# Order by destination stored without gaps, its gathers in a ring of 64 chunks: a four-layer graph network

## What is computed

```python
# layer 0: three hops, z = segment_sum(edge_weight * z[src], dst as rows) ...
# layer 1: 8 heads, softmax over the edges of each dst
e = (q[dst] * kt[edge_type, src]).sum(-1) * ...
a = softmax of e per dst;  agg = segment_sum(a * vt[edge_type, src], dst)
# layer 2: 4 heads, softmax per dst of att . leaky_relu(x_l[src] + x_r[dst])
out = segment_sum(alpha * x_l[src], dst)
# layer 3: 8 heads, scores q[src] . k[dst], softmax per src, sum per dst
weights = softmax of scores per src;  agg = segment_sum(v[src] * weights, dst)
```

## Time and profile before

| what | value |
|---|---|
| median of 3 runs | 13384.99 us (13377.65 to 13407.79) |
| profiled execution, span | 13177.8 us |
| its own time | not listed apart from the span; the median lies 207.2 us over the span |
| TensorE's mean granted clock | 0.635 of full speed |
| first gather of layer 1, 2, 3, weighing pass | 6900.7, 8566.2, 10202.1, 11693.4 us |
| last gather of the same | 8385.2, 10067.5, 11573.7, 13120.0 us |
| gathers of the same | 832, 832, 784, 832 |

### The profile page before, as it was taken

One profiled execution on the slowest core, in us unless ns is written; L12 is line 12 of the kernel. 1 busy time (PEld: TensorE's weight loads), 2 busy tenths in 40 slices (PEclk: granted clock), 3 DMA queues, 4 the chain that ended last, 5 costly groups with the idle time before them and its releaser, 6 DMA issues. The chain is left out here.

```text
span 13177.8 us, 169349 instructions
## 1 busy us (share of the span) xinstructions
PE 6872.9 (52%) x37679; PEld 6012.4 (46%) x37680; DVE 6549.5 (50%) x22663; ACT 2082.2 (16%) x6208; POOL 7027.7 (53%) x7417
## 2 busy tenths in 40 slices
PE   5555444445554555100384555656666566665555
PEld 4444333335554555100234455456665465654444
DVE  6444455555555555200265555755556344455555
ACT  4222100001110111000121111311222111122222
POOL 6555566646664666777205555245553555535554
PEclk6555555556666666555687777877787555556766
DMA  0000011111111111010143222111112211112232
GB/s 19 1 1 1 21 44 44 44 42 42 42 43 40 42 42 43 16 22 8 50 157 79 74 74 74 56 38 39 39 39 65 52 38 38 38 47 77 79 81 74
DMA packets 436083, 614.60 MB, mean 47 GB/s; under 512 B 176625, under 2 KB 312133, under 8 KB 435173
## 3 DMA queue, kind: packets, MB, share of 16 engines
q0 software_dynamic: 257024, 486.93, 14.5%
q1 hardware_dynamic: 178369, 119.49, 3.2%
q10 hardware_dynamic: 292, 3.41, 0.1%
HBM read 520.17 MB, written 89.19 MB: 46 GB/s over the span
## 5 line engine op out<-in xcount | busy, mean ns | idle before, releaser
L1094 POOL DMA_INDIRECT hop_rows<-hops,k_src_gather x1568 | 1479.3, 943 | 1077.3 <-issue 435.9
L1137 PE MATMUL hop_sums<-hop_rows,hop_weighted 128*128 x4992 | 1159.9, 405 | 1110.7 <-DVE k_x L1184 736.1
L1137 PEld LDWEIGHTS hop_sums<-hop_rows,hop_weighted 128*128 128x128 f32 x4992 | 1009.7, 300 | 1201.7 <-issue 1200.4
L1443 POOL DMA_INDIRECT l_pass_rows<-related,k_dst_typed x832 | 786.2, 945 | 1216.8 <-POOLq L74 517.6
L1443 POOL DMA_INDIRECT l_pass_rows<-left_table,k_dst_other x832 | 786.6, 945 | 895.7 <-DVE l_pass_terms L1815 490.5
L1938 POOL DMA_INDIRECT l_weigh_rows<-row_table,l_weigh_ring x832 | 813.0, 977 | 733.8 <-ACT l_weigh_ring L1902 466.3
L1443 POOL DMA_INDIRECT l_pass_rows<-key_table,k_src_gather x784 | 739.5, 943 | 766.6 <-DVE l_pass_scores L1752 387.3
L726 POOL DMA_INDIRECT src_sorted<-src_scatter_records,src_scatter_places x784 | 750.6, 957 | 606.3 <-DVE src_scatter_places L714 393.6
L1538 PE MATMUL l_pass_sums<-l_pass_zero 128*128 128x272 bf16 (+1 forms) x1210 | 262.7, 306 | 1454.0 <-DVE l_total L1632 1005.2
L1094 POOL DMA_INDIRECT hop_rows<-in_x,k_src_gather x784 | 739.6, 943 | 456.4 <-issue 220.8
L1292 POOL DMA_INDIRECT dst_sorted<-rec,dst_places x784 | 809.2, 1032 | 262.1 <-issue 262.1
(11 more groups left out here) (467 smaller groups left out, 18342.8 us busy)
## 6 DMA issues: line engine op xcount, KB each, us to landing
related<-l_tables_rows SPq DMA_DIRECT2D x50, 1024.0 KB, 4.4
hop_rows<-hops,k_src_gather POOLq DMA_INDIRECT x1568
l_pass_rows<-related,k_dst_typed POOLq DMA_INDIRECT x832
l_pass_rows<-left_table,k_dst_other POOLq DMA_INDIRECT x832
l_weigh_rows<-row_table,l_weigh_ring POOLq DMA_INDIRECT x832
src_sorted<-src_scatter_records,src_scatter_places POOLq DMA_INDIRECT x784
hop_rows<-in_x,k_src_gather POOLq DMA_INDIRECT x784
dst_sorted<-rec,dst_places POOLq DMA_INDIRECT x784
```

Source lines behind the costliest of these rows:

```text
L1094: nc.gpsimd.indirect_dma_start(rows[:, s * G + g, :], None, table_in, bass.IndirectOffsetOnAxis(ap=o.gather[:, c:c + 1], axis=0),).then_in ...
L1137: last = nc.tensor.matmul(sums[:, b, g, :], weighted[:, s % SLOTS, g, :], rows[:, bass.ds(slots[g], 1), :], start=True, stop=True)
L1443: nc.gpsimd.indirect_dma_start(rows[:, s, g, :], None, table, bass.IndirectOffsetOnAxis(ap=index[:, c:c + 1], axis=0),).then_inc(got[s], 16)
```

## The change

The order by destination is placed by `place_edges` too, without gaps, and read by a new `read_sorted`, which picks place and begins of the columns by masks. Layers 1 and 2 and the weighing pass then gather 784 chunks into a ring of 16 batches. Chunks of a group are no longer neighbours in the ring, so each engine that reads them loads four places and works chunk by chunk: DVE for pairs, terms and the weighing pass's subtraction, ACT for layer 2's copy, PE for layer 2's matmul with the gathered rows. The waits on `got` become waits on `landed` by a loaded count. `o.release` holds, for each batch, after how many groups its ring place is free; POOL loads it and waits for that many terms. In the weighing pass POOL's loop is unrolled, ACT's copy of indices goes, and SP is added. Layer 3's softmax pass and the hops stay as they are. The diff, cut to its core:

```diff
--- before.py
+++ after.py
@@ place_edges, tensor @@
+        if o.release is not None:
...
@@ place_edges, vector (its end) @@
+        if o.release is not None:
+            chain(nc.vector.tensor_scalar(bound[:], o.chunk_no[0:TU, 0:2], float(G), float(G), ALU.mult, ALU.add))
+            below = column_no[0:TU, :]
+            for h in range(2):
...
+            dve.wait_ge(pe_step, 5)
+            chain(nc.vector.tensor_scalar(upto_i[:], upto_rows, float(G - 1), None, ALU.add))
+            nc.vector.tensor_single_scalar(o.release, upto_i[96:97, :], 2, ALU.arith_shift_right)
@@ read_sorted (new, in place of read_order), tensor @@
+            for h in range(2):
+                pe.wait_ge(loaded[h], 16)
+                for f, out, done in ((1, turned, other_ok), (2, typed, typed_ok)):
+                    for q in range(here_q):
+                        last = nc.tensor.transpose(out[:, h, q * TU:(q + 1) * TU], by_edge[:, h * here_q + q, :, f],
+                                                   k.ident[0:TU, 0:TU])
+                    last.then_inc(done, 1)
+            pe.wait_ge(chosen_ok, 1)
+            pick_columns(nc, placed, zero, lambda q: by_edge[:, q, :, 0], chosen).then_inc(placed_ok, 1)
+            pe.wait_ge(found, 2)
+            pick_columns(nc, begun, zero, lambda q: starts[:, q, :], chosen).then_inc(begun_ok, 1)
...
@@ read_sorted, vector: 8 of these, then the fields @@
+                last = nc.vector.tensor_scalar(chosen[:, q, 0:hi - TU * q], o.chunk[0:TU, TU * q:hi], o.chunk_no[0:TU, q:q + 1],
+                                               None, ALU.is_equal)
+            last.then_inc(chosen_ok, 1)
...
@@ -1317,10 +1281,9 @@
-    ring = lag + 1 if values_at is not None else RING if ringed else 4
     with ExitStack() as ctx:
         sb, ps, sem = tools(nc, k, ctx, name)
-        rows = sb("rows", [P, ring, G, row])
+        rows = sb("rows", [P, RING * G, row])
@@ softmax_pass, sync @@
-            for n in range(GU if ringed else 0):
+            for n in range(GU):
                 sp.wait_ge(got[n % RING], (n // RING + 1) * 16 * G)
                 sp.sem_inc(landed, 1)
@@ softmax_pass, gpsimd @@
-            for n in range(GU if ringed else GROUPS):
-                s = n % ring
-                if n >= ring:
-
-                    pool.wait_ge(weighed if at else scored, n - ring + 1 + (NBLK // G if ringed else 0))
+            for n in range(GU):
+                s = n % RING
+                if n >= RING:
+
+                    if o.release is None:
+                        pool.wait_ge(scored, n - RING + 1 + NBLK // G)
+                    else:
+                        upto = pool.value_load(o.release[:, n - RING:n - RING + 1], min_val=1, max_val=GROUPS)
+                        pool.wait_ge(weighed, upto)
                     pool.sem_inc(running, 1)
                 for g in range(G):
                     c = n * G + g
-                    nc.gpsimd.indirect_dma_start(rows[:, s, g, :], None, table,
+                    nc.gpsimd.indirect_dma_start(rows[:, s * G + g, :], None, table,
                                                  bass.IndirectOffsetOnAxis(ap=index[:, c:c + 1], axis=0),
                                                  ).then_inc(got[s], 16)
@@ softmax_pass, scalar @@
-                    nc.scalar.copy(pair[:, t % 2, :, :, head:deep].rearrange("p g h a -> p g (h a)"),
-                                   rows[:, t % ring, :, D:D + heads]).then_inc(joined, 1)
+                    slots_of = load_blocks(nc, act.engine, o.slot[:, t * G:(t + 1) * G], G, RING * G - 1)
+                    for g in range(G):
+                        last = nc.scalar.copy(pair[:, t % 2, g:g + 1, :, head:deep].rearrange("p g h a -> p g (h a)"),
+                                              rows[:, bass.ds(slots_of[g], 1), D:D + heads])
+                    last.then_inc(joined, 1)
@@ softmax_pass, tensor @@
-                        pe.wait_ge(got[t % ring], (t // ring + 1) * 16 * G)
+                        slots_of = load_blocks(nc, pe.engine, o.slot[:, t * G:(t + 1) * G], G, RING * G - 1)
+                        need = pe.value_load(o.need[:, t:t + 1], min_val=1, max_val=GU)
+                        pe.wait_ge(landed, need)
                     for g in range(G):
...
-                            last = nc.tensor.matmul(own[:, b, g, :], k.ident[:], rows[:, t % ring, g, 0:D],
+                            last = nc.tensor.matmul(own[:, b, g, :], k.ident[:], rows[:, bass.ds(slots_of[g], 1), 0:D],
                                                     start=False, stop=True)
                     last.then_inc(spread_ok, 1)
@@ -1706,25 +1678,19 @@
                 if 0 <= t < GROUPS:
                     b = t % 2
 
-                    if ringed:
+                    if att is None:
                         slots_of = load_blocks(nc, dve.engine, o.slot[:, t * G:(t + 1) * G], G, RING * G - 1)
                         need = dve.value_load(o.need[:, t:t + 1], min_val=1, max_val=GU)
                         dve.wait_ge(landed, need)
-                    else:
-                        dve.wait_ge(got[t % ring], (t // ring + 1) * 16 * G)
                     dve.wait_ge(spread_ok, t + 1)
                     if t >= 2:
                         dve.wait_ge(scored, t - 1)
-                    if ringed:
-                        by_chunk = rows[:].rearrange("p r g f -> p (r g) f")
+                    if att is None:
                         for g in range(G):
                             last = nc.vector.tensor_tensor(pair[:, b, g:g + 1, :, :].rearrange("p g h f -> p g (h f)"),
-                                                           own[:, b, g:g + 1, :], by_chunk[:, bass.ds(slots_of[g], 1), :],
+                                                           own[:, b, g:g + 1, :], rows[:, bass.ds(slots_of[g], 1), 0:D],
                                                            ALU.mult)
                         last.then_inc(paired, 1)
-                    elif att is None:
-                        nc.vector.tensor_tensor(pair[:, b, :, :, :].rearrange("p g h f -> p g (h f)"), own[:, b, :, :],
-                                                rows[:, t % ring, :, 0:D], ALU.mult).then_inc(paired, 1)
@@ softmax_pass, vector, the terms @@
+                    slots_of = load_blocks(nc, dve.engine, o.slot[:, m * G:(m + 1) * G], G, RING * G - 1)
                     if m >= 2:
                         dve.wait_ge(summed, m - 1)
-                    nc.vector.tensor_tensor(
-                        terms[:, m % 2, :, 0:D].rearrange("p g (h f) -> p g h f", h=heads),
-                        rows[:, m % ring, :, values_at:values_at + D].rearrange("p g (h f) -> p g h f", h=heads),
-                        held[:, c:c + G, :].rearrange("p g (h a) -> p g h a", a=1)
-                        .to_broadcast([P, G, heads, head]), ALU.mult).then_inc(weighed, 1)
+                    for g in range(G):
+                        last = nc.vector.tensor_tensor(
+                            terms[:, m % 2, g, 0:D].rearrange("p (h f) -> p h f", h=heads),
+                            rows[:, bass.ds(slots_of[g], 1), values_at:values_at + D].rearrange("p a (h f) -> p (a h) f", h=heads),
+                            held[:, c + g, :].rearrange("p (h a) -> p h a", a=1).to_broadcast([P, heads, head]), ALU.mult)
+                    last.then_inc(weighed, 1)
@@ weigh_and_sum, scalar: list_rows and its calls go @@
-            def list_rows(n, s):
-
-                act.wait_ge(weighed, n + 1)
-                nc.scalar.copy(ring[:, s, :], index[:, bass.ds(n * G, G)]).then_inc(listed, 1)
@@ weigh_and_sum, gpsimd @@
-            with pool.Fori(0, ROUNDS) as i:
-                for s in range(SLOTS):
-
-                    pool.wait_ge(listed, i * SLOTS + s + 1)
+            for n in range(GU):
+                s = n % RING
+                if n >= RING:
+
+                    upto = pool.value_load(o.release[:, n - RING:n - RING + 1], min_val=1, max_val=GROUPS)
+                    pool.wait_ge(weighed, upto + SLOTS)
                     pool.sem_inc(running, 1)
-                    for g in range(G):
-                        nc.gpsimd.indirect_dma_start(rows[:, s, g, :], None, table,
-                                                     bass.IndirectOffsetOnAxis(ap=ring[:, s, g:g + 1], axis=0),
-                                                     ).then_inc(got[s], 16)
+                for g in range(G):
+                    c = n * G + g
+                    nc.gpsimd.indirect_dma_start(rows[:, s * G + g, :], None, table,
+                                                 bass.IndirectOffsetOnAxis(ap=index[:, c:c + 1], axis=0),
+                                                 ).then_inc(got[s], 16)
+
+        @block.sync
+        def _(sp):
+            for n in range(GU):
+                sp.wait_ge(got[n % RING], (n // RING + 1) * 16 * G)
+                sp.sem_inc(landed, 1)
@@ weigh_and_sum, vector @@
```

(46 more changed lines are left out.)

297 lines of the change are left out of this document (120 added, 177 removed).

## The result

The changed kernel takes 13559.0 us (median of 4 runs) where the kernel before takes 13387.1 on the same chip: ratio 1.0126, 95% interval 1.0114 to 1.0137. 13560 was forecast. The question is whether the terms were right or only their sum.

What follows compares the result with a forecast made beforehand. The prediction took a chain of waits to bound the kernel, gathering and computing taking turns. Fewer gathers, shown added work, and reading with placing summed as 13385 - 29 + 179 + 25 = 13560 us, range 13280 to 13830.

Steps and rivals of the forecast that it cites:

- reading: New reading of the sorted order: 40 matmuls and 8 masks, all on the path, +15 us.
- placing: Placing beside the next hop's fill: some 15 more DVE steps and 2 more PE rounds, 0 to +40, taken as +10 us.
- fills of 80 us with few groups: First ring fills of the passes: expected to last 80 us with only 2 to 4 groups scored.
- the tail of 15 groups: Weighing pass: some 15 groups expected to remain after its last gather.
- rival (a): Gathering passes: the period belongs to the batch, so 36 fewer batches save 253 us; 13235 us, chance 0.20.
- layer 3 pays 65.0 us of idle ... 0.41 us each: Layer 3's idle before its pairs in 157 batches, taken as the loading price in layers 1, 2 and weighing.
- The share of 0.3: Layers 1, 2 and weighing: part of the 597 us of added work expected to show, +179 us.
- The chain being serial in the weighing pass above all: Weighing pass: reason given in rival (c) for the added work showing in full, +597 us.
- Fewer gathers: Layers 1, 2 and weighing: 208 to 196 batches each, 2.2 us a batch; -16, -26 and +13, together -29 us.
- 4.84 us as the price of a group without gathers: Gathering passes: time of each group computed without a batch, read at layer 3's end.
- rival (c): Layers 1, 2 and weighing: the added work shows in full, +597 us; 13978 us, chance 0.12.
- 200 ns a register: Skill's price for register loads in layers 1, 2 and weighing: 27 x 0.2 x 208 = 1123 us before any overlap.

Runs made afterwards that it cites:

- four_ops: Changed kernel with one register loaded in place of four, batch places in layers 1, 2 and weighing, the four operations kept (wrong rows); ratio to before 1.0139.
- before again: Kernel before, unchanged, run and profiled a second time on another chip; span 13166.5 us, median 13177 us.
- dummy_loads: fewer_landed with unused register loads put back in layers 1 and 2; in layer 1 only need's load ran; ratio 0.9997, from 0.9944.
- fewer_landed: Kernel before with larger rings, 196 fixed-place batches in layers 1 and 2, and waits on landed; 13115.2 us, ratio 0.9944.
- one_op: four_ops with one operation over four chunks in place of four; slower: layer 2 gains 30 us, layer 1 and weighing lose 25 and 82.
- ahead: Changed kernel with its register loads placed ahead of waits and tables on partitions 0 and 32; 13474.4 us against 13552.3.
- fewer_loads: Changed kernel with layers 1 and 3 loading ahead, layer 1 reading need once in four groups, weighing tables in upper rows; ratio 1.0061.

## Why the forecast was right in its sum and wrong in its terms

By stage, with four_ops for the change (same ratio; the same kind of chip as before again), against my own terms by stage (the saving and 0.3 of the added work):

```
             forecast            measured
layer 1      -16 + 50 = +34      +137
layer 2      -26 + 60 = +34      +53
layer 3      0                   +4
weighing     +13 + 68 = +81      -18
reading      +15                 +6
placing      +10                 +14
sum          +175                +196 (runs: 13364.4 - 13176.6 = +188)
```

(The forecast's rows are rounded; unrounded they give 175.)

**What held.** 784 gathers, fills of 80 us with few groups, the tail of 15 groups (though the sum had 28 groups left there), 0.89 us for the four pairs, reading and placing (20 us for 25), and the view that gathers and computing hinder each other. By the runs a batch was worth 3.2 to 4.3 us, not 7.0, which refutes rival (a). The 0.12 us between two copies of one chunk stood in no row; the changed kernel's copies on ACT start 0.11 us apart. Placing went from 9.5 to 23 us and reading from 18 to 23. Of the two fields that the reading picks by 20 matmuls each, DVE waited 4.8 us for this one:

```profile
L687 PE MATMUL dst_read_placed<-dst_read_chosen,dst_read_lst x20: 275/450/570, 6974.5 to 6979.0; 98*128 98x147 f32 x10, 98*128 98x122 f32 x2, 98*128 98x25 f32 x2, 98*128 98x24 f32 x2
```

**What failed.**

1. The sentence "layer 3 pays 65.0 us of idle ... 0.41 us each", as the price of all loads of a group. It counts DVE idle that one place of one layer shows. What grew is the sequencer's work: from 0.47 to 2.69 us a group on DVE in layer 1 (4.25 loads of 0.44 us and 10.5 register operations for the dynamic places), from 1.09 to 3.2 in the weighing pass. So all the added work, which I had put at 0.81, 0.97 and 1.09 us, measured 1.71, 0.91 and 2.18 with the gathers left out. That the sequencer's part is what costs is shown for one load a group (dummy_loads) and, in the weighing pass, by DVE's waits; for the rest of layer 1's +137 us it is argued, since POOL's release and the uneven need came in together with it. Where layer 2's +53 come from isn't known: of the 94 us from fewer_landed to four_ops, one_op gives 30 back.
2. The share of 0.3 for all three passes. It was read from DVE's busy time in layers 1 and 3, where what decides is what stands in front of a wait: four_ops against fewer_landed in layer 1 is 0.70 us longer a group (7.67 against 6.97), most of the 0.81 that I had listed and 0.41 of the 1.71 measured alone; in layer 2 0.47 of 0.97 listed and 0.91 measured; in the weighing pass less than none.
3. "The chain being serial in the weighing pass above all": computing alone did grow by 2.18 us there, to 6.39, but the gathers then added almost nothing to it, so that 6.90 became 6.43. I had costed a stage as gathers plus a part of the computing, and didn't ask what happens when computing alone comes near the period. In that pass it fell to the larger of the two.
4. Fewer gathers: in layers 1 and 2 they are worth, rings paid, 13184.4 - 13110.7 = 74 us (76 by the stages against before again), where I had 42. The sum let every batch of the steady stretch carry one group; in the changed layer 1 702 gathers, 175.5 batches, go with 186 groups.
5. 4.84 us as the price of a group without gathers, read from layer 3's tail, is right for layer 3 (4.75) and was used for all; layer 1 takes 5.12 alone, not 3.8, a figure from groups that had been half done in the fill.

So by my prices rival (c) was near the mark in layer 1 and wrong for the rest, and the sum came out by errors of opposite sign: 103 us too little in layer 1 and 99 too much in the weighing pass. That it hit within 1 us is luck. The Trainium skill's 200 ns a register ("Runtime: NRT & Kernel Launch", Instruction fetch mechanics) is given there with the register loads that the runtime puts in; carrying it over to a kernel's loads from its own tables was my step, and these runs don't bear it out: a load of four registers took 0.35 us where one of one took 0.31.

The wait view of the weighing pass from 12180 to 13380 has DVE's own sequencer ("issue") as the one thing of weight that DVE waits for, 1.7 us a group:

```profile
POOL l_weigh_rows L1900 <- DVE l_weigh_terms L2015: 216.0, 68, 8.8
DVE l_weigh_pair L1986 <- issue: 196.2, 183, 1.4
DVE l_weigh_onehot L138 <- issue: 116.6, 183, 1.7
```

## What to carry to other kernels

Price a register load by where it stands: in front of a datapath that waits for it most of it shows (0.4 of 0.52 us a group in layer 1), moved under a running operation a part comes back (47 to 53 us of layer 3), and its count of registers matters little. Before adding work to a stage in which transfers and computing hinder each other, measure the computing alone: if it comes near the period, the stage can become bound by it, and taking work off that engine again may lose, as one_op did in the weighing pass (82 us). And compare profiles only after stages with unchanged code have shown that both come from equal chips.

## What the hardware showed that I had not expected

In these kernels a register load's time goes with which partition the one before read. In the changed kernel DVE's loads alternate between partition 0 and partitions 64 and 96: those that switch took 0.53 to 0.57 us, the others 0.31 to 0.35; with tables on partitions 0 and 32 all took 0.31 to 0.35. PE's two loads a group took 0.33 us with their tables on partitions 0 and 32, and 0.51 with the second on 64 (runs ahead and fewer_loads). Without gathers layer 3 became 0.26 us a group longer by it, with no line of its code changed; with gathers beside it, on chips of the first kind, by nothing (1447 to 1457 us against 1453), on the third by 35 us (1488 against 1453 in dummy_loads).

In the four passes PE's signals come late only where there are gathers: with the gathers left out none of them is late in either kernel. In layer 1 before the change the late ones lag by 4.2 us in the median, and come in the median 1.3 us after the end of the gather that POOL issued last; but in the changed weighing pass, where POOL is about as busy (656 of 1200 us against 739 of 1300), hardly any is late. What makes the difference stays open. So does why the same programs take 1.5% longer on one of the three chips, most of all in the scatter by source (1374 us against 1329).
